# A kernel of four layers on one core: fewer full products around the score-only slots and the end of its second attention, and another order of its last sigmoids

## The chip, the cores and the metric

The kernel runs on one core of one Trainium2 chip. TensorE multiplies matrices (its clock is granted at one of two levels, 1.2 or 2.4 GHz), VectorE and ScalarE work elementwise and reduce, GpSimd (POOL in the rows) is a slower helper, and SyncE queues the transfers. The engines run their own instruction streams and wait for each other on semaphores. The metric is the device time of one execution in microseconds (us), smaller is better.

## The reference

On x of 8 samples x 256 tokens x 128 features, four layers with residuals, each behind a layer norm:

```python
x = x + attn_a(layernorm(x))     # hyperbolic-distance attention, 16 heads of 8
x = x + ffn(layernorm(x))        # 64 experts of 64, 8 of them chosen per token, and a shared one
x = x + attn_b(layernorm(x))     # softmax attention with rotary positions, 16 heads of 8
x = x + ffn(layernorm(x))        # the same experts again
...
# attn_b, per sample and head: q, k rotated
attn = softmax(einsum('qd,kd->qk', q, k) * 8 ** -0.5)
out = attn @ v
...
# routing in ffn
scores = sigmoid(x @ router_w.T)         # then grouped top-k on scores + e_bias
w = chosen scores / their sum * 2.5
```

The change lies in attn_b and in the routing of the second ffn.

## The kernel before, in words

Everything stays in on-chip memory between layers. Phase b is attn_b. prepare_b makes q and k with rotary positions in four groups of 512 tokens and, with "selection" matmuls, spreads the heads over four groups of 32 partitions each (b_qt, b_kt), as a high and a low part. samples_b then walks over 64 units of two heads of one sample, B * UNITS = 64.

Each unit goes through two kinds of score tiles. As unit V its scores are computed query by key (b_score_step), 2 heads x 2 halves of 32 x 128 weights by 256 columns, into one of three score banks (0 to 2), and VectorE reduces each head's bank to the row maxima (tensor_reduce into mx, line L2284, counted by s_mx; the matmuls count up s_s1). Every four units the maxima go through GpSimd (max_split), a transpose and a selecting matmul on TensorE (b_max_step, lines L959 and L539), ScalarE and VectorE (shift, into q2, shown as q in the rows), which subtracts them from q. AHEAD = 9 slots later, as unit U = V - 9, the shifted scores are computed key by query (b_shifted_step) into banks 3 to 5, ScalarE takes their exp (L1450, counted by s_e), and three slots later TensorE multiplies with v (pv_b, rows ps<-wr,vt).

So TensorE's slots are of three kinds. V = 3 to 8 have scores only (U = -1); they are called the lead here. U = 0 to 54 have scores and shifted scores, in four row groups at once. U = 55 to 63 have shifted scores only, and U = 64 only closes; this is the tail. In the tail and behind it (last_of_b, b_tail_step) the second ffn's router logits, its transposes and the attention's last projections are mixed into TensorE's line in an order written out by hand; on VectorE the same is written out behind its loop over V in samples_b: x_low (low part of the normalised input), marks, normalise(2) (waits for heads reloaded by transfer), sigmoids (two steps on the logits' exponentials), the last shift, the routing steps.

keep_busy(n, k) issues k full products, 128 x 128 weights by 512 columns, into a bank whose content nobody reads. They stand ahead of the selection of the last q group (8 of them, behind the scores of V = 0), behind every lead slot (3), at U = 0 to 3 (1 each), at some V where TensorE waits for the residual path (WAITS_FOR_PATH), and in the tail (TAIL_FILL, 16 in all). In the rows they are ps<-sel. All matmuls come from a helper, so their line is L539.

Of the kernel before, what the change touches and what calls it, by code (L numbers as in the profile page):

```python
# [24 lines left out]
MT = N // P  # L25
# [14 lines left out]
AHEAD = QUAD + 5  # L40
# [53 lines left out]
def hybrid(nc, x, consts, wA, wB, bqk, brow, rwT, wexp, out):  # L94
    ctx = ExitStack()

    def sem(name):
        return ctx.enter_context(nc.semaphore(name))
# [5 lines left out]
    with ctx:  # L104
# [207 lines left out]
        s_s1 = sem("b_scores_in_psum")  # L312
        s_mx = sem("b_max_read")
# [76 lines left out]
        def shifted_bank(h):  # L390

            return 3 + h % 3
# [144 lines left out]
        def _(pe):  # L537
# [274 lines left out]
            def xn_transposed_b(g):  # L812

                pe.wait_ge(s_xn, GROUPS + g + 1)
                if g >= 1:
                    pe.wait_ge(s_u, 2 * g - 1)
                for t in range(GTILES):
                    last = pe.transpose(bank(2)[:, t * P:(t + 1) * P], b_xn[g % 2][:, t, :], ident)
                last.then_inc(s_xnT, 1)
# [34 lines left out]
            def prepare_b():  # L854
                keep_busy(0, 14)
                xn_transposed_b(0)
                project_b(0)
                values_b(0)
                xn_transposed_b(1)
                for g in range(GROUPS):  # L860
                    if g + 1 < GROUPS:
                        project_b(g + 1)
                    else:
                        pe.wait_ge(s_u, 2 * GROUPS)
                        pe.wait_ge(s_vc, 2 * GROUPS)
                        b_tiles(-1, 0)
                        keep_busy(3, 8)
                        b_score_head(1, 0)
                    select_q_b(g)
                    if g + 1 < GROUPS:  # L870
                        values_b(g + 1)
                    else:
                        b_score_head(1, 1)
                        b_score_head(2, 0)
                        b_score_head(2, 1)
                    if g + 2 < GROUPS:
                        xn_transposed_b(g + 2)
                    select_k_b(g)

            def keep_busy(n, k):  # L880

                for _ in range(k):
                    mm(bank(n), sel[:, S_QH].rearrange("p c r -> p (c r)"), sel[:, :].rearrange("p s c r -> p (s c r)"))
# [7 lines left out]
            def b_shifted_step(U, mt, i):  # L891
# [2 lines left out]
                return mm(bank(shifted_bank(2 * U + i))[:, mt * N:(mt + 1) * N], b_kt[rows(j0 + i), c, tok(s, mt * P, P)],  # L894
                          q2[U // UNITS % 2][rows(j0 + i), s % 4, :], tile_position=(32 * (j0 + i), 0))

            WAITS_FOR_PATH = {20: 3, 36: 4, 41: 3, 42: 4, 52: 4, 57: 3, 58: 4}
            TAIL_FILL = {55: 1, 56: 1, 57: 1, 58: 2, 59: 2, 60: 2, 61: 1, 62: 2, 63: 1, 64: 3}

            def b_tiles(U, V):  # L900

                shifted, scores = 0 <= U < B * UNITS, V < B * UNITS
                if V == 0:
                    pe.wait_ge(s_outL, 4 * GROUPS + 2)
                    pe.wait_ge(s_outR, 3 * GROUPS + 2)
                elif V == 4:
                    pe.wait_ge(s_outL, 4 * GROUPS + 4)
                    pe.wait_ge(s_outR, 3 * GROUPS + 4)
                elif V == UNITS:
                    pe.wait_ge(s_outL, 6 * GROUPS)  # L910
                    pe.wait_ge(s_outR, 5 * GROUPS)
                if shifted and U % (UNITS // 2) == 0:
                    pe.wait_ge(s_q2, U // (UNITS // 2) + 1)
                if shifted and U >= 2:
                    pe.wait_ge(s_e, 2 * U - 2)
                if 0 <= U < 4:
                    keep_busy(shifted_bank(2 * U), 1)
                elif V in WAITS_FOR_PATH:
                    keep_busy(shifted_bank(2 * U), WAITS_FOR_PATH[V])
                elif U in TAIL_FILL:  # L920
                    keep_busy(shifted_bank(2 * U) if U <= 61 else 0, TAIL_FILL[U])
                for i in range(2):
                    if scores and 2 * V + i >= 3:
                        pe.wait_ge(s_mx, 2 * V + i - 2)
                    if shifted and i == 1 and U >= 1:
                        pe.wait_ge(s_e, 2 * U - 1)
                    for half in range(MT):
                        if scores:
                            last = b_score_step(V, half, i)
                            if half == MT - 1:  # L930
                                last.then_inc(s_s1, 1)
                        if shifted:
                            last = b_shifted_step(U, half, i)
                            if half == MT - 1:
                                last.then_inc(s_s2, 1)
# [54 lines left out]
            def samples_b():  # L990
                for V in range(3, AHEAD):
                    b_tiles(-1, V)
                    b_max_step(V)
                    keep_busy(3, 3)
                for U in range(B * UNITS + 1):
                    V = U + AHEAD
                    b_tiles(U, V)
                    if U == B * UNITS:
                        pv_b(B * UNITS // 2 - 1, 0)
                        pv_b(B * UNITS // 2 - 1, 1)  # L1000
                    elif U >= 3:
                        pv_b((U - 3) // 2, (U - 3) % 2)
                    if U == B * UNITS - 1:
                        pv_b(B * UNITS // 2 - 2, 1)
                    elif U == 55:
                        pe.wait_ge(s_mx, 2 * B * UNITS - 1)
                        logits(1, 0, 0)
                    b_max_step(V)
                    if V < B * UNITS:
                        b_path_step(V)  # L1010
                    else:
                        b_tail_step(U)
# [799 lines left out]
        def _(dve):  # L1812
# [125 lines left out]
            def sigmoids(f, i, g=None):  # L1938

                sc = route[f].sc[i] if g is None else route[f].sc[i][:, g * GTILES:(g + 1) * GTILES, :]  # L1940
                dve.wait_ge(s_sc, lap(f, i, 1 if g is None else g))
                if f == 0:
                    dve.wait_ge(s_S, CHUNKS * B - 1)
                step(dve.tensor_scalar(sc[:, :, :], sc[:, :, :], BIG, 1.0, ALU.min, ALU.add))
                step(dve.reciprocal(sc[:, :, :], sc[:, :, :]))
# [76 lines left out]
            def marks(f):  # L2022
                st.do(dve.memset(route[f].gs[:, :, 8:12], BIG))

            def x_low(f, i, g):

                dve.wait_ge(s_xh, lap(f, i, g))
                dve.tensor_tensor(xl[:, group(i, g)], f_xT[2 * i + g][:, :], xh[:, group(i, g)],
                                  ALU.subtract).then_inc(s_xl, 1)
# [249 lines left out]
            def samples_b():  # L2279
# [7 lines left out]
                def shift(k):  # L2287
                    s, half = k // 2, k % 2
                    dve.wait_ge(s_mq, k + 1)
                    if s >= 2:  # L2290
                        dve.wait_ge(s_s2, 2 * UNITS * (s - 1))
                    cs = slice(2 * half, 2 * half + 2)
                    first, chunk, _ = unit_b(UNITS * s + 4 * half)
                    dve.tensor_tensor(q2[s % 2][:, cs, :], bank(7).rearrange("p (c n) -> p c n", c=2),  # L2294
                                      b_qt[:, chunk, tok(first, 0, 2 * N)].rearrange("p (c n) -> p c n", c=2),
                                      ALU.add).then_inc(s_q2, 1)

                def normalise(c):
                    dve.wait_ge(s_old, 64 * (c + 1))
                    den = b_rden[c % 2][:, :, :].rearrange("p r j -> p j r")  # L2300
                    st.do(dve.reciprocal(den, b_rows[:, :, HD, :]))
                    st.sync()
                    if c >= 2:
                        dve.wait_ge(s_oT, B + c - 1)
                    dve.tensor_tensor(b_otok[c % 2][:, :, :].rearrange("p j (r d) -> p j r d", d=HD),  # L2305
                                      b_rows[:, :, 0:HD, :].rearrange("p j x r -> p j r x"),
                                      den.unsqueeze(3).broadcast_to([P, 4, 16, HD]), ALU.mult).then_inc(s_on, 1)
# [47 lines left out]

                x_low(1, 0, 0)
                marks(1)
                normalise(2)
                sigmoids(1, 0, 0)
                shift(2 * B - 1)  # L2360
                x_low(1, 0, 1)
                sigmoids(1, 0, 1)
                route_bests(1, 0)
                residual(2, 1)
                stats_of(2)
# [171 lines left out]
```

## Time and profile before

| what | value |
|---|---|
| median of 3 runs | 1074.56 us |
| the three runs | 1070.37, 1074.8, 1074.56 us |
| the profiled execution's own time | 1078.8 us |
| its span, first to last instruction | 1077.0 us |
| TensorE matmuls busy | 970.0 us (90%) |
| VectorE busy | 961.2 us (89%) |
| ScalarE busy | 673.4 us (63%) |
| GpSimd busy | 375.3 us (35%) |
| mean granted TensorE clock | 0.868 |

The profile is of one execution. Busy times are unions of an engine's instruction times; matmuls are pipelined, so a matmul's recorded time holds its way through the array too, and two of them overlap. A granted clock of 1.00 is 2.4 GHz and 0.50 is 1.2 GHz; a stretch's figure is the mean over it. All times in rows count from the span's start.

### The profile page before, as it was taken

How to read it: one execution, taken by the hardware profiler on the slowest of the kernel's cores; microseconds unless marked ns; L12 is line 12 of the kernel's file. 1: busy time of each engine (PE TensorE's matmuls, PEld its weight loads, DVE VectorE, ACT ScalarE, POOL GpSimd, SP SyncE). 2: the span in 40 equal slices, each digit the busy share in tenths (PEclk: the TensorE clock that was granted, in tenths of full speed). 3: DMA queues.
4: the chain of work that ended last, by engine and by line, in shares of the span. 5: the costliest groups of instructions: out<-in, count | busy, mean ns of one | idle time of the engine just before them, and what ended most of it. 6: DMA issues, size and time to landing. Idle time of an engine off the chain costs nothing. (4 is left out here: it accounts for less than half of the span.)

```text
span 1077.0 us, 17673 instructions
## 1 busy us (share of the span) xinstructions
PE 970.0 (90%) x5412; PEld 694.4 (64%) x5412; DVE 961.2 (89%) x1448; ACT 673.4 (63%) x855; POOL 375.3 (35%) x300
## 2 busy tenths in 40 slices
PE   6767888787669999999999899999999999999997
PEld 4543444444347888888888645455678888888885
DVE  7789999999988999999999797998889999999996
ACT  4779999999934545545454555877544545455453
POOL 3044666668811333334332141111203333333330
PEclk9865555555669999999999997999989999999999
DMA  2000000000108755565551000111059555555521
GB/s 59 0 2 1 1 1 1 1 1 1 52 11 201 181 150 153 151 156 143 159 148 33 1 1 1 24 24 24 23 125 230 144 158 149 153 153 151 155 69 39
DMA packets 50711, 86.94 MB, mean 81 GB/s; under 512 B 20092, under 2 KB 33404, under 8 KB 50556
## 3 DMA queue, kind: packets, MB, share of 16 engines
q1 hardware_dynamic: 50664, 86.34, 31.3%
q8 instruction: 27, 0.44, 0.2%
q14 instruction: 20, 0.16, 0.1%
HBM read 83.33 MB, written 2.98 MB: 80 GB/s over the span
## 5 line engine op out<-in xcount | busy, mean ns | idle before, releaser
L1547 ACT ACTIVATE sg<-ps 128x512 f32<-128x512 f32 x264 | 156.9, 594 | 266.2 <-PE ps L539 265.4
L539 PE MATMUL ps<-xh,whi 128*128 128x512 f32 x528 | 206.8, 392 | 1.3 <-ACT b L1366 1.3
L539 PE MATMUL ps<-xh,wlo 128*128 128x512 f32 x528 | 206.3, 391 | 0.0
L539 PE MATMUL ps<-xl,whi 128*128 128x512 f32 x528 | 206.2, 390 | 0.0
L2077 DVE TENSOR_TENSOR hf<-sg,ps 128x512 f32<-128x512 f32 x264 | 170.6, 684 | 30.0 <-DVE hl L2396 24.4
L1768 POOL CAST whi<-wraw 128x384 fp32r<-128x384 f32 x66 | 66.0, 1000 | 364.0 <-PE ps L539 285.6
L1687 POOL TENSOR_TENSOR rr<-xr,rr 128x2048 f32<-128x2048 f32 x32 | 145.2, 4568 | 125.4 <-ACT rr L1341 71.1
L2396 DVE TENSOR_TENSOR hl<-hf,hh 128x1024 fp32r<-128x1024 f32 x132 | 178.8, 1355 | 0.5 <-DVE hf L2077 0.5
L2401 DVE TENSOR_TENSOR hf<-hf,cbc 128x1024 f32<-128x1024 f32 x128 | 157.0, 1227 | 13.4
L1553 ACT ACTIVATE hh<-hf 128x1024 fp32r<-128x1024 f32 x132 | 139.1, 1054 | 4.3 <-DVE hf L2401 4.3
L1770 POOL TENSOR_TENSOR wlo<-wraw,whi 128x384 fp32r<-128x384 f32 x66 | 116.4, 1763 | 5.3
L539 PEld LDWEIGHTS ps<-xh,whi 128*128 128x128 f32 x528 | 99.7, 189 | 22.6 <-ACT b L1366 1.4
L539 PEld LDWEIGHTS ps<-xh,wlo 128*128 128x128 f32 x528 | 99.6, 189 | 21.0
L539 PEld LDWEIGHTS ps<-xl,whi 128*128 128x128 f32 x528 | 99.7, 189 | 20.7
L539 PE MATMUL ps<-hh,whi 128*128 128x512 f32 x264 | 104.2, 395 | 4.2 <-DVE hl L2396 4.2
L539 PE MATMUL ps<-hh,wlo 128*128 128x512 f32 x264 | 103.6, 392 | 0.0
L539 PE MATMUL ps<-hl,whi 128*128 128x512 f32 x264 | 103.5, 392 | 0.0
L2284 DVE TENSOR_REDUCE mx<-ps 128x2 f32<-128x512 f32 x128 | 81.1, 683 | 12.5 <-PE ps L539 11.6
L2108 DVE TENSOR_SCALAR xr<-ps 128x1024 f32<-128x1024 f32 x64 | 77.8, 1216 | 10.3 <-PE ps L539 7.4
L1450 ACT ACTIVATE wr<-ps 128x512 f32<-128x512 f32 x128 | 69.5, 599 | 27.3 <-PE ps L539 26.6
L539 PE MATMUL ps<-rr,vt 128*32 128x256 f32 x512 | 67.4, 631 | 17.0 <-ACT rr L1323 17.0
L2116 DVE SCALAR_TENSOR_TENSOR xr<-ps,xr 128x1024 f32<-128x1024 f32 x64 | 78.1, 1221 | 4.3 <-PE ps L539 0.3
(276 smaller groups left out, 1525.3 us busy)
## 6 DMA issues: line engine op xcount, KB each, us to landing
cbc<-routing_coefficients SPq DMA_DIRECT2D x256, 256.0 KB, 3.8
wraw<-in_wexp_dram SPq DMA_DIRECT2D x66, 192.0 KB, 2.7
X<-in_x_dram SPq DMA_DIRECT2D x4, 256.0 KB, 4.4
routing_coefficients<-cT SPq DMA_DIRECT2D x8, 128.0 KB, 2.3
out_dram<-X SPq DMA_DIRECT2D x4, 256.0 KB, 2.9
heads_by_row<-o_all SPq DMA_DIRECT2D x12, 72.0 KB
b_rows<-heads_by_row SPq DMA_DIRECT2D x12, 72.0 KB, 3.0
rope_in<-in_consts_dram SPq DMA_DIRECT2D x1, 512.0 KB, 3.5
```

The costliest lines, as they stand in the source:

```text
L539: return pe.matmul(o, l, r, start=start, stop=stop, **kw)
L1450: act.activation(wr[:, C % CHUNKS, h % 4 * MT * N:(h % 4 + 1) * MT * N], bank(shifted_bank(h)), ACT.Exp, scale=SCALE_B).then_inc(s_e, 1)
L1547: act.activation(sg[c % 2][:, :], bank(4 + 2 * (c % 2)), ACT.Silu).then_inc(s_sg, 1)
L1553: act.activation(hh[ring][:, :], hf[ring % 2][:, :], ACT.Copy).then_inc(s_hh, 1)
L1687: pool.tensor_tensor(rr[:, C % RR, :], xr[:, C % XR, :], rr[:, C % RR, :], ALU.add).then_inc(s_S, 1)
L1770: pool.tensor_tensor(wlo[slot][:, :], wraw[raw][:, :], whi[slot][:, :], ALU.subtract).then_inc(s_ws, 1)
L2077: dve.tensor_tensor(hf[c // 2][:, c % 2 * FF_TOK:(c % 2 + 1) * FF_TOK], sg[c % 2][:, :], bank(5 + 2 * (c % 2)), ALU.mult).then_inc(s_h1, 1)
L2108: dve.tensor_scalar(xr[:, C % XR, at], bank(0, 2), 0.0, None, ALU.max).then_inc(s_N, 1)
L2116: dve.scalar_tensor_tensor(xr[:, C % XR, at], bank(2, 2), R_MAX, xr[:, C % XR, at], ALU.min, ALU.mult).then_inc(s_X, 1)
L2284: dve.tensor_reduce(mx[U // UNITS % 2][:, c, j0 + i, :], bank(score_bank(2 * U + i)).rearrange("p (t m) -> p t m", t=MT), AX_X, ALU.max).t ...
L2396: dve.tensor_tensor(hl[ring][:, :], hf[ring % 2][:, :], hh[ring][:, :], ALU.subtract).then_inc(s_hl, 1)
L2401: dve.tensor_tensor(hf[side][:, :], hf[side][:, :], cbc[s][:, side * FF_PAIR:(side + 1) * FF_PAIR], ALU.mult).then_inc(s_h, 1)
```

## The change

It edits four places. Ahead of the last q selection, 5 full products stand instead of 8. Behind each lead slot, 2 instead of 3 (LEAD_FILL). In lead slots, both heads now wait together until the maxima up to head 2V - 2 are read, and their matmuls are issued half by half, heads by turns; before, each head waited for itself and its two halves were issued in a row. In the tail TAIL_FILL loses entries: one product less at U = 56, 57, 59 and 60, two less at U = 62. On VectorE, the sigmoids of the first logit group stand ahead of normalise(2), and those of the second ahead of x_low of that group.

```diff
                         b_tiles(-1, 0)
-                        keep_busy(3, 8)
+                        keep_busy(3, 5)
                         b_score_head(1, 0)
...
+            LEAD_FILL = {V: 2 for V in range(3, AHEAD)}
             WAITS_FOR_PATH = {20: 3, 36: 4, 41: 3, 42: 4, 52: 4, 57: 3, 58: 4}
-            TAIL_FILL = {55: 1, 56: 1, 57: 1, 58: 2, 59: 2, 60: 2, 61: 1, 62: 2, 63: 1, 64: 3}
+            TAIL_FILL = {55: 1, 58: 2, 59: 1, 60: 1, 61: 1, 63: 1, 64: 3}
...
+                if scores and not shifted and V >= 3:
+                    pe.wait_ge(s_mx, 2 * V - 1)
+                    for half in range(MT):
+                        for i in range(2):
+                            last = b_score_step(V, half, i)
+                            if half == MT - 1:
+                                last.then_inc(s_s1, 1)
+                    return
                 for i in range(2):
                     if scores and 2 * V + i >= 3:
                         pe.wait_ge(s_mx, 2 * V + i - 2)
...
                     b_max_step(V)
-                    keep_busy(3, 3)
+                    keep_busy(3, LEAD_FILL.get(V, 0))
...
                 marks(1)
+                sigmoids(1, 0, 0)
                 normalise(2)
-                sigmoids(1, 0, 0)
                 shift(2 * B - 1)
+                sigmoids(1, 0, 1)
                 x_low(1, 0, 1)
-                sigmoids(1, 0, 1)
                 route_bests(1, 0)
```

## Rows read from the trace of the kernel before

**Rows 1.** The page's costliest groups: count, then busy us, mean ns, idle before.
```profile
L1450 ACT ACTIVATE wr<-ps 128x512 f32<-128x512 f32 x128 | 69.5, 599 | 27.3 <-PE ps L539 26.6
```

**Rows 2.** Busy time by stretch: us, engines (instructions), granted clock, DMA, GB/s.
```profile
core 0: us, PE busy (x) PEld busy (x) DVE busy (x) ACT busy (x) POOL busy (x), PEclk, DMA share, GB/s
639.30:643.00 3.70, 3.70 (x18) 2.39 (x16) 3.49 (x5) 1.07 (x3) 0.86 (x1) 0.66 0.02 4
...
645.20:647.00 1.80, 1.58 (x12) 0.96 (x12) 1.11 (x2) 1.80 (x2) 1.49 (x1) 1.00 0.00 0
...
656.06:658.37 2.31, 2.31 (x8) 1.34 (x8) 1.29 (x2) 0.00 (x0) 0.12 (x1) 0.50 0.00 0
...
661.07:664.00 2.93, 2.76 (x31) 1.92 (x30) 2.39 (x4) 2.34 (x5) 0.00 (x0) 1.00 0.00 0
...
683.48:689.22 5.74, 5.41 (x68) 2.68 (x69) 5.56 (x10) 5.00 (x11) 0.70 (x5) 1.00 0.02 4
749.30:767.15 17.85, 17.84 (x164) 10.03 (x163) 13.18 (x30) 13.41 (x28) 3.13 (x7) 1.00 0.27 48
```

**Rows 3.** Timeline of the lead: start us, us, engine, line, count [idle before].
```profile
639.81 3.21 PE L539 MATMUL ps<-sel 128*128 128x512 f32 x8
...
641.31 0.69 DVE L2249 TENSOR_TENSOR b_kl<-rope,b_kh 128x512 fp32r<-128x512 f32 x1
...
642.96 0.80 PE L539 MATMUL ps<-b_qh,sel 32*128 32x512 f32 x3
...
645.24 0.50 PE L539 MATMUL ps<-b_kh,sel 32*128 32x512 f32 x2 [0.21 <-ACT b_qt L1390]
...
646.72 0.39 PE L539 MATMUL ps<-b_kt,b_qt 32*128 32x256 f32 x4
...
648.40 0.80 PE L539 MATMUL ps<-b_kt,b_qt 32*128 32x256 f32 x4
...
649.12 1.65 PE L539 MATMUL ps<-sel 128*128 128x512 f32 x3
649.23 1.29 DVE L2284 TENSOR_REDUCE mx<-ps 128x2 f32<-128x512 f32 x2 [0.79 <-PE ps L539]
...
659.10 2.05 PE L539 MATMUL ps<-sel 128*128 128x512 f32 x4
```

**Rows 4.** Timeline of TensorE, narrow windows inside one lead slot.
```profile
658.37 0.58 PE L539 MATMUL ps<-b_kt,b_qt 32*128 32x256 f32 x2
...
658.75 0.42 PE L539 MATMUL ps<-b_kt,b_qt 32*128 32x256 f32 x2
```

**Rows 5.** The chain that ended last, in order: start us, us, what.
```profile
652.12 9.47 PE ps L539 x33
...
685.13 0.37 PE ps L959 x2
...
759.88 9.28 PE ps L539 x89
```

**Rows 6.** Timeline of the tail, columns as in rows 3.
```profile
751.75 0.47 PE L539 MATMUL ps<-sel 128*128 128x512 f32 x1
751.98 0.38 ACT L1481 ACTIVATE sc<-ps 128x256 f32<-128x256 f32 x1
752.16 0.51 PE L539 MATMUL ps<-q,b_kt 32*128 32x256 f32 x4
...
754.15 0.56 DVE L2301 RECIPROCAL b_rden<-b_rows 128x64 f32<-128x64 f32 x1 [3.50 <-DMA b_rows<-heads_by_row]
...
755.68 0.29 DVE L1944 TENSOR_SCALAR sc<-sc 128x256 f32<-128x256 f32 x1
...
757.80 0.69 DVE L2294 TENSOR_TENSOR q<-ps,b_qt 128x512 fp32r<-128x512 f32 x1
...
759.23 0.66 PE L1023 MATMUL ps<-cst,b_otok 128*128 128x128 f32 x4
...
763.64 0.71 PE L539 MATMUL ps<-sel 128*128 128x512 f32 x2
764.28 0.51 PE L539 MATMUL ps<-q,b_kt 32*128 32x256 f32 x4
...
765.28 0.50 PE L539 MATMUL ps<-sel 128*128 128x512 f32 x1
```

## The prediction

> **What bounds the kernel now.** I read the page first for what phase b costs TensorE, VectorE and ScalarE [rows 1], then the stretches with their granted clock [rows 2], the order of time at the start of phase b [rows 3], the chain that ended last [rows 5] and the order of time in its last slots [rows 6]. The reader is to see three regimes.
>
> In the lead, the six slots with scores only (V = 3 to 8), TensorE never rests, the granted clock is 0.50, that is 1.2 GHz, and VectorE is busy 1.29 us of a slot of 2.31 us (the row from 656.06 is one slot [rows 2]). VectorE idles 0.79 us before a pair of maxima; TensorE has 0.80 us of scores in a slot and 1.65 us of three full products [rows 3]. So the lead is bound by its own fillers at the low clock. It lasts from 646.72 to 661.07, 14.35 us. The chain of work shows it as one piece of TensorE, 9.47 us [rows 5]. From U = 0 on the clock is 1.00 and four slots take 5.74 us; VectorE is busy 5.56 us of them, TensorE 5.41 [rows 2], but TensorE could do its own in about 4.7 (below), so VectorE binds. In the tail (U from 55) there are no scores to reduce; TensorE is busy 17.84 of 17.85 us, fillers included, at full clock [rows 2], and the chain is TensorE's for 9.28 us on end [rows 5]. The experts behind it begin when the routing behind the tail is done, so what the tail gives goes to the end.
>
> **The change part by part.**
>
> *Ahead of the selection, eight products become five.* They begin at 639.81 and the next matmuls start at 642.96 [rows 3]. A full product is 512 columns, 0.427 us at 1.2 GHz; the rows agree, as four take 2.05 us and three 1.65 [rows 3]. Three of them are 1.28 us. But the selection of q behind them also waits for b_kl on VectorE, which ends 0.69 us after 641.31, at 642.00, so it can move up only by about 0.91 us, from 642.96 to 642.05 [rows 3]. Next in line is ScalarE's copy of b_qt, which follows the selection. On the other side: the clock in 639.3 to 643.0 is 0.66 on the mean and it is 1.00 in 645.2 to 647.0 [rows 2]; it fell during the eight products and rose after them. With three fewer, and an idle wait for b_kl, I don't expect it to rise there. The selections of k and the scores of V = 3, now 645.24 to 646.72 at full clock [rows 3], and the short V = 3 slot (646.72 to 648.40, 1.68 us, against 2.31) then run at half. I price that at 1.0 us (0.5 for two selections and the scores, which stream 0.5 us and would stream twice that; 0.2 for the three fillers' part of the slot; the rest for the copies in between). Bounds: 0 if it rises anyway, 1.5 if all 1.48 us from 645.24 on double. Net of this part: 0.1 us later, between 0.9 earlier and 0.6 later.
>
> *Two products in each lead slot instead of three.* Six slots, 0.427 us each, TensorE bound: 2.56 us. Is there something that takes their place? VectorE needs 1.29 us, and the slot left is 1.88 us, so no. The new wait for all maxima up to head 2V-2 stands before both heads and behind it on TensorE are the scores, the transposes of the maxima and the fillers. It ends with the first maximum of the slot before, 0.83 + 0.69 us after that slot's scores began (649.23 less 648.40, and one of two in 1.29 us, rounded up) [rows 3]: 1.52 against 1.88, hidden by 0.36. At full clock it would be what sets the pace, at 1.3 us a slot. The shift of q that U = 0 waits for ends with VectorE's work of V = 6, three slots ahead; free.
>
> *Heads by turns.* Worth nothing. In the narrow look at one lead slot two score matmuls have started at 658.37 and cover 0.58 us together, two more cover 0.42 us from 658.75 [rows 4]: two and two, side by side, which fits one of each head, in its own row group. The Trainium skill (TensorE: Matmul & The Clock Gate, Part 3, The mechanism) says that a weight load overlaps matmuls in flight only if it goes to another row group, and that matmuls keep their order; by that rule the order of before, two matmuls of one row group in a row, should have cost up to one such step a slot, and turns should save it (rival D). The trace of before does not bear this out, as the pairs start together.
>
> *The tail, six products fewer* (16 to 10, counted in the diff: one each at U = 56, 57, 59, 60, two at 62). The sole product of a slot delays its shifted scores from 751.75 to 752.16, 0.41 us; two delay them from 763.64 to 764.28, 0.64 us, so the second is 0.23 [rows 6]. Sum: 0.41 + 0.41 + 0.23 + 0.23 + 0.64 = 1.92 us, if no wait takes over. ScalarE's two exps are 1.2 us a slot [rows 1] and the slots stay at 1.4 and more, because each also has transposes, logits or a projection. The next wait is U = 59: transposed(2) and U = 60 wait for the last shift, which runs at 757.80 for 0.69 us behind the reciprocal of the sigmoids; TensorE comes to it at 759.23 [rows 6], and 1.05 us earlier (0.41 + 0.41 + 0.23) that would be 758.18, 0.3 us too soon. That is what the new order on VectorE cures: it idles 3.50 us until the row load lands at 754.15 [rows 6], and the first sigmoids, 2.1 us (755.68 to 757.80), now fit into this gap, since their logits have been exponentiated by 752.36 [rows 6]. The shift then ends at about 756.8. x_low of group 1 moved behind the second sigmoids is not asked for until the experts; free, hidden by the wait for the projection. All of the 1.92 us count; bounds 1.2 (one wait of about 0.7 us back) and 2.2.
>
> *What the low clock does afterwards.* In the trace of before the clock came back at U = 0 (0.50 until 661, then 1.00 [rows 2]), just after four products in a row, 2.05 us [rows 3]. Now there are three there and two in each slot before it, while slots with three stayed at 0.50 here. I expect U = 0 to start at the low clock. A steady slot is at full clock 1.00 us of shifted scores and products with v (764.28 to 765.28 [rows 6]; the scores run beside the shifted ones in other row groups), and in four slots there are 0.37 us of transposed maxima [rows 5] and about as much of their selection: 4.7 us. At 1.2 GHz the scores of a slot take 0.73 us (648.40 to 649.12 [rows 3]) where a slot of the tail has about 0.43; by a ratio of 1.75 (between 1.7 and 2) the four slots take 8.2 us, against 5.74: 0.6 us a slot, TensorE then being the bound. The first three slots have no product with v and lose about 0.3 us together. From U = 3 on TensorE is nearly gapless and the clock should return within some slots; no row shows when. Nearest above is the three products at V = 20, U = 11. I take three costly slots, 0.3 + 1.8 = 2.1 us; bounds 0 (returns as before) and 0.3 + 8 x 0.6 = 5.1.
>
> **Sum**: +0.1 - 2.56 - 1.92 + 2.1 = -2.3 us. The profiled execution took 1078.8 us, 4.2 above the median of 1074.56; the runs of before span 4.4 us, much as a lead at the low or at the full clock would, so I make the sum against the profiled execution, 1076.5, and carry the difference to the median: 1072.3, said as 1072. Its own range: all bounds at their best -0.9 - 2.56 - 2.2 = -5.7, at their worst +0.6 - 2.56 - 1.2 + 5.1 = +1.9, so 1069 to 1076.5. About 0.5%, 5.4 us, is what a measurement of this kernel tells from no change: the forecast is a small gain that would not count as faster.
>
> **Rivals.** (A) The lead at full clock. If five and two products suffice to hold 2.4 GHz, VectorE sets the slot at 1.3 us: six slots 7.8 us instead of 14.35, 6.5 us saved, with 0.9 ahead and 1.9 in the tail 9.3 us. 1074.6 less 9.3 is 1065.3; as some runs of before may have had the full clock there too, I say 1066. For it: the slots get shorter, and TensorE's real work in them comes more often. Against it: TensorE was gapless in 648.4 to 661.07 and yet at 0.50 [rows 2], and two selections with copies between them, where it waits, stand just ahead. Chance 0.2.
> (B) The low clock stays, the other side. One mechanism: with fewer products the steady slots at 1.2 GHz feed the engine no more than the lead did, and the clock doesn't return until a group of fillers (V = 20, 36). Each slot costs 0.6 us; it eats the 4.4 us gain after about 7 slots, and from 16 slots on the kernel is slower by over 0.5%. Until V = 20: +1 us, 1075; until V = 36 (U = 27): 0.3 + 24 x 0.6 = 14.7, less 4.4, 1085. Chances 0.09 and 0.05.
> (C) Order within the tail: a wait takes the products' place (for exp of the slot before, or the row load for normalise, if it lands late), and the tail gives 0 to 1 us: 0.1 - 2.56 - 0.5 + 2.1 = -0.9 in all, 1073.7. Chance 0.11.
> (D) The turns do shorten the scores. The second halves start 0.38 us after the first [rows 4]; were one such step saved in each of six slots, it would be 2.3 us more: 1070. Against it: two of the four have started together already. Chance 0.05. The rule of the Trainium skill above is what speaks for it.
> The forecast keeps 0.50.
>
> **How the numbers follow.** Faster by over 0.5% (below 1069.2): most of A (0.18), half of D (0.02), and the forecast where the clock returns early (0.12): 0.32. Slower by over 0.5% (above 1079.9): late B, 0.05, and 0.02 for runs with it half the time: 0.07. The rest, 0.61, is within. The range takes in A's 1066 and early B's 1075 with the spread of the runs themselves: 1065.5 to 1077.5; late B and the far end of A, some 0.15, are left out.
>
> **What would show it.** In the profile of after: lead slots 1.9 us apart at clock 0.50 (right), 1.3 apart at 1.00 (A); the first slots from U = 0 about 2 us apart at 0.50, and where the clock returns; VectorE's idle time before its maxima down to about 0.4 us; the tail from 749.3 to 767.15 shorter by 1.9, with the shift ended before TensorE asks. It makes the prediction wrong above all if the clock behaves otherwise at U = 0, in either direction.

## The result and the profile after

The changed kernel takes 1082.11 us at the median of 13 runs (1072.86 to 1083.4), the kernel before 1074.56 us at the median of its 13 (1069.57 to 1082.1). The ratio is 1.0045, with an interval of 1.0024 to 1.0065. By the 0.5% used above that is not a clear loss, but its interval lies above 1: the gain of 2.3 us that was forecast isn't there. The profiled execution took 1083.4 us (span 1081.6), 4.6 us more than the profiled one of before (1078.8, span 1077.0). Ratios in this document leave out runs over 1.5% above a kernel's fastest; this matters for one experiment and is said there.

The page's group of the exps is as in [rows 1], now at line 1459; the change moves the lines below it by nine:

```profile
L1459 ACT ACTIVATE wr<-ps 128x512 f32<-128x512 f32 x128 | 69.5, 598 | 31.9 <-PE ps L539 31.1
```

Busy time by stretch, to be held against [rows 2]; the columns are the same:

```profile
639.30:643.00 3.70, 3.18 (x19) 1.90 (x19) 3.70 (x6) 1.22 (x2) 1.55 (x1) 1.00 0.02 4
...
653.26:655.13 1.87, 1.87 (x7) 1.00 (x6) 1.46 (x3) 0.00 (x0) 0.00 (x0) 0.50 0.00 0
661.10:664.00 2.90, 2.90 (x26) 1.64 (x25) 2.73 (x6) 1.72 (x5) 0.64 (x4) 0.50 0.00 0
664.44:672.92 8.48, 8.41 (x74) 3.68 (x70) 5.79 (x10) 5.27 (x11) 0.70 (x4) 0.50 0.01 2
684.50:690.24 5.74, 5.40 (x72) 2.68 (x68) 5.55 (x9) 4.88 (x11) 0.70 (x4) 1.00 0.00 0
...
755.07:771.41 16.34, 16.33 (x158) 9.37 (x156) 13.21 (x28) 13.41 (x28) 3.75 (x7) 1.00 0.28 53
...
644.20:681.60 37.40, 37.33 (x223) 19.63 (x223) 25.19 (x40) 17.86 (x31) 5.29 (x21) 0.50 0.00 1
681.60:705.50 23.90, 21.34 (x273) 10.55 (x266) 22.81 (x37) 20.16 (x40) 2.10 (x12) 1.00 0.22 26
```

The reader is to see the row from 644.20: 37.40 us at 0.50, the lead and eleven slots behind it, with TensorE busy for 37.33 us of it. In the kernel before, the low clock ended at U = 0. From 639.3 to 643.0 the granted clock is 1.00 now; in the kernel before its mean there was 0.66. Four slots with both kinds of scores take 8.48 us in it (the row from 664.44, U = 4 to 7) and 5.74 at full clock (from 684.50), and VectorE, which binds at full clock, is busy only 5.79 of the 8.48. The tail's stretch (from 755.07) is 16.34 us long instead of 17.85.

The timeline of the lead, TensorE and VectorE, columns as in [rows 3]:

```profile
639.12 1.43 PE L539 MATMUL ps<-sel 128*128 128x512 f32 x5
...
641.41 0.52 PE L539 MATMUL ps<-b_qh,sel 32*128 32x512 f32 x4 [0.42 <-issue]
...
646.89 0.79 PE L539 MATMUL ps<-b_kt,b_qt 32*128 32x256 f32 x4
647.62 1.22 PE L539 MATMUL ps<-sel 128*128 128x512 f32 x2
648.77 0.79 PE L539 MATMUL ps<-b_kt,b_qt 32*128 32x256 f32 x4
...
655.86 1.65 PE L539 MATMUL ps<-sel 128*128 128x512 f32 x3
```
```profile
647.72 1.29 DVE L2293 TENSOR_REDUCE mx<-ps 128x2 f32<-128x512 f32 x2 [0.59 <-PE ps L539]
```

A plain lead slot runs from 646.89 to 648.77, 1.88 us, as forecast, and VectorE's idle time ahead of its maxima is 0.59 us ("about 0.4" was forecast). Here TensorE waited 0.42 us behind the five products, before it selected q; the row names no releaser, but b_kl was done at 641.31, 0.10 us ahead of the selection's start. The clock was 1.00 then and 0.50 from 644 on.

The chain of work (start, us, what) is TensorE's from 644.17 to 686.15 but for 0.07 us; three of its pieces ahead of U = 11 are these ([rows 5]):

```profile
650.18 8.06 PE ps L539 x28
658.86 7.40 PE ps L539 x47
666.88 4.96 PE ps L539 x36
```

The timeline of the tail ([rows 6]), with the shift's chain on VectorE:

```profile
757.65 0.50 PE L539 MATMUL ps<-q,b_kt 32*128 32x256 f32 x4
...
758.50 1.75 DVE L1954 RECIPROCAL sc<-sc 128x256 f32<-128x256 f32 x1
...
760.29 0.56 DVE L2310 RECIPROCAL b_rden<-b_rows 128x64 f32<-128x64 f32 x1
...
761.85 0.68 DVE L2303 TENSOR_TENSOR q<-ps,b_qt 128x512 fp32r<-128x512 f32 x1
...
764.20 0.66 PE L1032 MATMUL ps<-cst,b_otok 128*128 128x128 f32 x4
```

The first sigmoids now run ahead of the row load's reciprocal, and the shift ends at 762.53, 1.67 us before TensorE transposes.

Where the time went is best read by stages. This table is worked out from the starts of the first score matmul of a slot (V) or its first shifted one (U) in each profile; the stages that are left out (up to V = 0, and behind U = 63) make up the rest of the span. All times are in us.

```
kernel                       V0-V3  V3-U0  U0-U4  U4-U11 U11-U27 U27-U55 U55-U63  span
before                        7.35  14.36   5.27   10.61   25.55   47.25   15.96  1077.0
after                         6.49  12.25   7.01   16.65   26.89   47.55   14.44  1081.6
three in the lead             6.99  14.81   5.26   10.61   25.55   47.28   14.45  1074.4
eight ahead                   7.34  12.02   5.95   10.61   25.55   47.24   14.45  1075.6
tail only                     7.34  14.37   5.27   10.60   25.54   48.42   14.45  1079.4
turns only                    7.34  10.27   5.27   10.60   25.54   47.28   15.96  1072.9
four at U = 0                 6.97  11.43   5.27   10.60   25.53   47.27   14.44  1070.8
none at V = 20                6.44  12.26   7.01   11.12   26.10   47.27   14.45  1075.6
no turns                      6.31  12.29   7.01   12.10   25.53   47.26   14.45  1075.8
waits filled, three           7.97   8.66   5.27   10.60   26.62   47.57   14.44  1072.3
waits filled, two             7.97   8.29   5.27   10.60   26.78   47.54   14.45  1070.4
waits filled, and the path    7.97   8.29   5.27   10.60   24.66   46.40   14.45  1067.7
  and the route               7.96   8.29   5.26   10.61   24.66   46.38   14.44  1067.6
tail's table, old order       6.41  12.51   5.27   10.61   25.55   47.26   14.89  1072.0
```

After less before: 0.68 less up to V = 0, which is not the change's; 0.86 less to V = 3, 2.11 less in the lead, 1.52 less in the tail. That is 4.5 us given. Against it stand 1.74 more in U = 0 to 3, 6.04 more in U = 4 to 10, 1.34 and 0.30 more from there to U = 55, and 0.34 behind the tail: with the 0.68 the sum is +4.6. So the gain came where it was expected, 4.5 us, and the stages with the low clock behind the lead (U = 0 to 10) took 7.78 us.

Most of the 1.34 have their own place: 0.24 us is the first slot from U = 11, in which the clock came back, and 1.09 us is the slot U = 26, where at V = 35 TensorE waits for the path. The timeline there, first of after and then of before:

```profile
705.39 0.95 PE L1032 MATMUL ps<-cst,b_otok 128*128 128x128 f32 x4 [1.55 <-DVE b_otok L2314]
705.99 2.05 PE L539 MATMUL ps<-sel 128*128 128x512 f32 x4
```
```profile
701.02 0.63 PE L1023 MATMUL ps<-cst,b_otok 128*128 128x128 f32 x4 [1.57 <-DVE b_otok L2305]
701.40 1.17 PE L539 MATMUL ps<-sel 128*128 128x512 f32 x4
```

The clock fell to 0.50 at 705.5, just behind the end of the wait, and the four products there took 2.05 us instead of the 1.17 that they take at full clock. The same wait before (1.57 us) had no such fall in its profile. The 0.30 us from U = 27 to U = 55 are the end of the same low stretch, which lasted until 709.

### The profile page after: what moved, and what is told of

The parts are those of the page before. It is cut to its first block and busy times, and to the rows that moved or that the text cites. A ratio compares the mean times of both kernels' runs of the same rounds, so it can differ in the third digit from the quotient of the medians.

```text
span 1081.6 us, 17644 instructions
## 1 busy us (share of the span) xinstructions
PE 975.0 (90%) x5397; PEld 693.3 (64%) x5397; DVE 962.9 (89%) x1448; ACT 673.9 (62%) x855; POOL 376.9 (35%) x300
```

## The experiments

Each has twelve runs, but for the last, which has one; each is named as in the table. They were taken in three sets, on three different chips: first the four of the next section; then four at U = 0, none at V = 20 and the two with the waits filled; then the rest. Every ratio is to runs of the kernel before in the same set, whose medians were 1074.98, 1075.03 and 1074.98 us.

For every single run the record also has the mean granted clock of the whole execution. It goes with the time: before's fastest runs of each set (1069.3 to 1069.7 us) have 0.878 or more, its runs above 1080 us 0.870 or less; the changed kernel has 0.871 at 1072.86 us and 0.857 to 0.862 in its eight runs above 1080.

### One part of the change undone, or done alone

**Three in the lead**: the changed kernel with the old number of products there.

```diff
-            LEAD_FILL = {V: 2 for V in range(3, AHEAD)}
+            LEAD_FILL = {V: 3 for V in range(3, AHEAD)}
```

> The changed kernel with three full products behind each lead slot again (five ahead, turns, tail and VectorE order as changed). Theory L (the low clock is carried past U = 0 because the lead has two products): the clock returns at U = 0 as in the kernel before, U = 0 to 11 take about 16 us instead of 23.7, and with the tail's 1.5 us the time is 1072 to 1074 us. Rival T (turns and the wait for both heads cost the time): about 1081 us, as the changed kernel.

Measured: 1075.22 us (1072.83 to 1080.43), ratio 0.9996 (0.9975 to 1.0018). The low clock lasted from 641 to 661.5 in its profile, so the lead was slow, but it was gone at U = 0, and U = 0 to 10 are as before (15.9 us, as expected). The time is 1.2 us above the 1072 to 1074 expected. The third figure from the right is the granted clock:

```profile
648.80:660.00 11.20, 11.20 (x38) 7.05 (x38) 6.13 (x10) 1.04 (x2) 1.33 (x8) 0.50 0.00 0
...
662.60:668.00 5.40, 4.99 (x54) 2.85 (x53) 5.40 (x10) 4.65 (x11) 0.70 (x4) 1.00 0.01 3
```

**Eight ahead**: the changed kernel with the old number ahead of the selection.

```diff
-                        keep_busy(3, 5)
+                        keep_busy(3, 8)
```

> The changed kernel with eight products ahead of the q selection again, all else as changed. Theory L with the lead's products as the cause: no better than the changed kernel, 1079 to 1082 us, the clock at 0.50 until V = 20. Theory L with the five ahead as the cause: the clock is 1.00 for part of the lead and at U = 0, 1073 us. Rival T: 1081 us, but with the clock back early.

Measured: 1077.17 us (1071.77 to 1082.18), ratio 1.0008 (0.9979 to 1.0036). The clock came back at 662.5, 2.0 us behind U = 0 (660.5), and U = 0 to 3 took 0.68 us more than before. The time lies between the two that were expected, and neither expectation had the clock as it came. Undoing either part gives most of the loss back, so neither part alone explains it.

**Tail only**: the kernel before with the tail's table and VectorE's new order.

```diff
-            TAIL_FILL = {55: 1, 56: 1, 57: 1, 58: 2, 59: 2, 60: 2, 61: 1, 62: 2, 63: 1, 64: 3}
+            TAIL_FILL = {55: 1, 58: 2, 59: 1, 60: 1, 61: 1, 63: 1, 64: 3}
...
-                normalise(2)
                 sigmoids(1, 0, 0)
+                normalise(2)
...
-                x_low(1, 0, 1)
                 sigmoids(1, 0, 1)
+                x_low(1, 0, 1)
```

> The kernel before with the tail's six products fewer and the new order of the sigmoids alone. Theory L: 1.5 us faster than before, 1073 us, and the clock in the lead and at U = 0 as before. Rival R (the tail or the order on VectorE costs time): not faster than before, 1075 us or more.

Measured: 1075.45 us, ratio 1.0011 (0.9988 to 1.0034). The tail took 14.45 us instead of 15.96, 1.51 less, in this profile as in all with the new table and the new order. The total doesn't show it: runs of one kernel differ by more, and a gain of 1.5 us would be a ratio of 0.9986, just outside the interval. In this profile a further low stretch, from 731.7 to 735.1, made U = 27 to 54 1.17 us longer.

**Turns only**: the kernel before with the heads by turns and their shared wait.

> The kernel before with heads by turns and the one wait for both heads in the lead slots alone (three products, eight ahead, tail as before). Theory L: no difference within 1 us, lead slots 2.3 us apart as before. Rival T: 3 to 7 us slower, with lead slots longer than 2.3 us. Rival D of the prediction (turns shorten the scores): up to 2.3 us faster, lead slots about 1.9 us apart.

Measured: 1074.59 us, ratio 0.9995 (0.9976 to 1.0015). In its profile the clock came back in the middle of the lead and the lead took 10.27 us, but a lead with three products and without turns also varied, between 14.37 and 12.51 us (tail only; tail's table, old order). The slot V = 4, at 0.50 almost throughout, took 2.28 us with turns, against 2.30 before. No effect of the turns is shown.

### How long the low clock lasts

**Four at U = 0**: the changed kernel, with four products in U = 0 instead of one.

```diff
-                    keep_busy(shifted_bank(2 * U), 1)
+                    keep_busy(shifted_bank(2 * U), 4 if U == 0 else 1)
```

> The changed kernel with four full products instead of one at U = 0, so that six stand in a row there (two of V = 8, four of U = 0). Theory L: three more products cost about 1.3 us at the low clock, and the clock comes back within U = 0 to 4 instead of at V = 20: U = 4 to 11 take 10.6 us instead of 16.7, and the time is 1075 to 1077 us. Rival (the low clock isn't what costs, but the order and waits of the lead): 1.3 us or more slower than the changed kernel, 1082 us and over.

Measured: 1075.75 us (1071.88 to 1077.99), ratio 0.9989 (0.9962 to 1.0016). Of the changed kernel's 13 runs 8 are above 1080 us, of these 12 none is above 1078, and none has a mean clock below 0.865. Its profile can't show the four products at work, since in that execution the clock had come back in the lead, on TensorE instructions that are those of the changed kernel up to there; only the times and mean clocks speak for the four products. (The kernel before has 8 of 34 runs above 1080 us in this set, so such times do occur on this chip.) The stretches of its profile:

```profile
645.00:650.00 5.00, 5.00 (x20) 2.87 (x18) 3.07 (x6) 3.97 (x4) 2.66 (x5) 0.50 0.00 0
650.00:655.00 5.00, 5.00 (x21) 3.04 (x20) 3.51 (x6) 0.38 (x1) 0.00 (x0) 0.54 0.00 0
655.00:660.00 5.00, 4.67 (x35) 2.90 (x31) 4.11 (x8) 1.37 (x4) 0.71 (x4) 1.00 0.00 0
```

It came back at 654.6.

**None at V = 20**: the changed kernel without the three products there (U = 11).

```diff
-            WAITS_FOR_PATH = {20: 3, 36: 4, 41: 3, 42: 4, 52: 4, 57: 3, 58: 4}
+            WAITS_FOR_PATH = {36: 4, 41: 3, 42: 4, 52: 4, 57: 3, 58: 4}
```

> The changed kernel without the three full products at V = 20 (U = 11). Theory L, that it is this group which brings the clock back in the profile of the changed kernel: the clock stays at 0.50 beyond 682 us, to the four products at V = 36 (U = 27) at the worst, at 0.8 us a slot: up to 13 us slower than the changed kernel, 1083 to 1094 us, with U = 11 to 27 up to 13 us longer. Rival (the clock returns by itself about there, products or not): 1 us faster than the changed kernel, 1080 us.

Measured: 1080.7 us (1072.07 to 1094.61), ratio 1.0001 (0.9957 to 1.0044); five of its twelve runs lie at 1089.0 to 1094.6 us and are not in the ratio. They are what matters here: no run of the changed kernel is above 1083.4, and these five have mean clocks of 0.841 to 0.849, where the changed kernel has 0.857 at the least. So without the three products at V = 20 the low clock lasted longer in some executions; how long, no profile shows. But they are not always needed. In the profile of this kernel it came back at 668.7:

```profile
660.00:665.00 5.00, 5.00 (x40) 2.64 (x36) 4.34 (x8) 3.37 (x7) 0.70 (x4) 0.50 0.00 0
665.00:670.00 5.00, 5.00 (x50) 2.37 (x52) 3.30 (x6) 2.68 (x6) 0.00 (x0) 0.63 0.02 3
670.00:675.00 5.00, 4.66 (x61) 2.21 (x53) 4.70 (x9) 4.62 (x10) 0.70 (x4) 1.00 0.00 0
```

Up to that place TensorE's instructions are those of the changed kernel, where it came back at 681.6. When it returns thus differs between executions of the same instructions.

**No turns**: the changed kernel, its two products a lead slot kept, with the old lead loop (each head waits for itself).

> The changed kernel without the heads by turns and without their shared wait; everything else as in the change. Theory L, that two products in each score slot are what leaves the granted clock at 0.50 until V=20, expects the stages from V=0 to U=11 as in the changed kernel, 42.4 us together, and some 1080 us. Theory T, that the turns are what keeps TensorE's clock low, expects the clock back near U=0, the stage from U=4 to U=11 at 10.6 us and some 1075 us.

Measured: 1079.36 us (1071.07 to 1082.32), ratio 1.0021 (0.9994 to 1.0047); 6 of 12 runs above 1080. V = 3 to U = 4 are as in the changed kernel (12.29 and 7.01 us), with the clock at 0.50; it came back at 668.8 in this profile. The clock stays low without the turns too. That the stages to U = 11 would be as long as in the changed kernel (42.4 us) did not come true in this execution: they took 37.7.

### Holding the full clock

**Waits filled, three**: before's numbers of products, the new tail, and products where TensorE waits between the selections. **Waits filled, two**: the changed kernel with eight ahead and the same products in the waits. The first three lines stand between the halves of select_k_b, for the last two groups of tokens, the last line behind the scores of V = 2's second head.

```diff
+                if g >= GROUPS - 2:
+                    pe.wait_ge(s_u, 2 * GROUPS)
+                    keep_busy(3, 2)
...
                         b_score_head(2, 1)
+                        keep_busy(3, 4)
```

> The kernel before with the changed tail and VectorE order, eight ahead and three in each lead slot, and with full products in the waits ahead of the lead, where TensorE idles: two between the halves of the k selections of groups 2 and 3, four behind the scores of V = 2. Theory L: the clock stays at 1.00 from 637 us through the lead, VectorE sets the lead slots at 1.3 us, V = 3 to U = 0 takes 8 us instead of 14.4, and the time is 1067 to 1070 us. Rival (the clock falls in the lead whatever stands ahead): 1073 to 1075 us, lead slots 2.3 us apart at 0.50.

> The changed kernel (two products in lead slots, turns, tail) with eight ahead and the same products in the waits ahead of the lead. Theory L: if the clock is at 1.00 when the lead begins, slots of 1.3 us with two products hold it there, as its slots are then short: 1067 to 1070 us, no different from three in each slot. Rival (two are too few at any clock): it falls in the lead, comes back only at V = 20, 1080 us.

Measured: with three 1074.03 us, ratio 0.998 (0.9953 to 1.0008); with two 1072.19 us (1069.87 to 1074.58), ratio 0.996 (0.9933 to 0.9988). In both profiles the clock is 1.00 throughout the lead, which takes 8.66 and 8.29 us instead of 14.36 and 12.25. The stretches and the timeline of the one with two:

```profile
647.00:655.40 8.40, 7.42 (x49) 4.18 (x45) 7.77 (x13) 2.87 (x4) 1.42 (x8) 1.00 0.00 0
...
695.00:699.00 4.00, 3.70 (x24) 2.57 (x24) 1.52 (x4) 0.67 (x2) 0.71 (x4) 0.57 0.00 0
```
```profile
648.36 0.50 PE L539 MATMUL ps<-b_kt,b_qt 32*128 32x256 f32 x4 [0.21 <-DVE mx L2297]
...
654.05 0.50 PE L539 MATMUL ps<-b_kt,b_qt 32*128 32x256 f32 x4 [0.68 <-DVE mx L2297]
```

Two things are to be seen. At full clock and with two products the lead is VectorE's: TensorE waits for the maxima. (With three, TensorE was busy for 8.00 of the 8 us from 648, and the lead is 0.37 us longer.) And with two products a slot the clock stayed at 1.00, as it did with three. But it fell at 695.2, behind the wait at V = 35, with three at 696.4. The clock and the lead came as expected, the times didn't, by 2 to 4 us (1067 to 1070 was expected for both): U = 11 to 26 took 1.23 and 1.07 us more than before, and V = 0 to 2, where the new products stand, 7.97 us instead of 7.34, though at full clock. So those products were not free. And of the twelve runs with three, two still took 1079.65 and 1081.2 us, at a mean clock of 0.868 and 0.869.

**Waits filled, and the path**: six products stand in that wait, at V = 35 and at V = 51, and the four in the score stream behind each are gone. **And the route**: nine products instead of three ahead of the last logits, and two behind them.

```diff
-            WAITS_FOR_PATH = {20: 3, 36: 4, 41: 3, 42: 4, 52: 4, 57: 3, 58: 4}
+            WAITS_FOR_PATH = {20: 3, 41: 3, 42: 4, 57: 3, 58: 4}
...
                     pe.wait_ge(s_q2, V // QUAD)
+                    pe.wait_ge(s_e, 2 * (V - AHEAD))
+                    keep_busy(shifted_bank(2 * (V - AHEAD + 1)), 6)
                     pe.wait_ge(s_on, B + c + 1)
```

> As the kernel of this batch with both parts, but with the part at V=35 and V=51 alone. My theory expects about 1.8 us from the eight products taken off the path and about 1.1 from the low stretch near 695 us: 1069 to 1070 us, and 1.00 granted from the first score slot to the end of the score stage. The rival (the products in the wait push the scores behind them) expects about 1072 us.

> The changed kernel with eight slots ahead and products in the waits of the selection, as in the run before this one of that kind (1072.2 us), and in addition: at V=35 and V=51 six products stand in the wait that VectorE's score path already has (about 1.6 us idle there) instead of four in the middle of the score stream, and the last projection matmuls of the route have nine products ahead of them instead of three and two behind (idle 1.6 and 0.8 us). My theory, that the granted clock falls to 0.50 after waits of TensorE and that every product on the path costs its own time, expects about 1.8 us from the eight products taken off the path, about 1.1 from the low stretch near 695 us that goes, and 0.5 to 1.5 from one low stretch less at 777 to 784: 1067.5 to 1070 us. The rival, that products in a wait delay what follows them as much as they give back, expects about 1072 us, no gain on that kernel.

Measured: with the path alone 1070.17 us (1069.39 to 1071.26), ratio 0.9939 (0.9915 to 0.9962), the lowest median here, and faster than before by its interval. The gain is in the median: before's fastest run of that set took 1069.46 us, about as long as the fastest with the path (1069.39), but its runs go up to 1082.41 and these only to 1071.26. It is 1070.43 us (1069.33 to 1074.29) with the route as well, ratio 0.9955 (0.9929 to 0.9981). The path came as expected, the route is worth nothing: the low stretch from 783.4 stands in both profiles. U = 11 to 55 took 71.06 us against 74.32 without this part, 3.3 less. The profile of before, with no low stretch at that place and the same fillers, took 72.80; so about 1.7 us of it goes with the eight products that are off the path, and about 1.5 with the low stretch. The timeline shows both:

```profile
693.42 1.65 PE L539 MATMUL ps<-sel 128*128 128x512 f32 x6
695.09 0.63 PE L1036 MATMUL ps<-cst,b_otok 128*128 128x128 f32 x4
```
```profile
693.88 1.06 DVE L2320 TENSOR_TENSOR b_otok<-b_rows,b_rden 128x512 f32<-128x512 f32 x1
```
```profile
695.00:699.00 4.00, 3.98 (x51) 2.33 (x54) 3.70 (x7) 3.01 (x6) 0.70 (x4) 1.00 0.00 0
```

The transposes start right behind the sixth product, 0.15 us after b_otok is there (694.94), as long after it as without the products (0.14 us in the kernel with two), and the scores behind them run at once and at full clock.

**Tail's table, old order**: the kernel before with the new TAIL_FILL and VectorE's old order of sigmoids, one run. (It is six products fewer, not five.)

> The kernel before with only the five full products less at the end (the table for U=56 to 62), and VectorE's old order of the last sigmoids. The prediction's step said that in this order the shifts would bind where products are gone. That expects the stage from U=55 to U=63 at 14.75 us or more, against 14.45 in the run that had both edits and 15.96 before. The rival, that the order of the sigmoids doesn't matter, expects 14.45.

Measured: 14.89 us for U = 55 to 62, against 14.45, and 1073.86 us in its one run. The timeline names the wait:

```profile
756.47 0.66 PE L1023 MATMUL ps<-cst,b_otok 128*128 128x128 f32 x4 [0.37 <-DVE q L2294]
```

The transposes of U = 59 wait 0.37 us for the last shift. The old order costs 0.44 us of the tail here.

## Why the prediction was wrong

Forecast were 1072 us, within 1065.5 to 1077.5; measured were 1082.11.

**The step that failed** is "I take three costly slots, 0.3 + 1.8 = 2.1 us". The mechanism up to there was the right one: U = 0 starts at the low clock, and a steady slot then is TensorE's. What failed is how soon the clock returns, and what a slot costs until then. The clock stayed low for eleven slots in the profiled execution, up to the three products at V = 20; this is rival B's first case, which had a chance of 0.09 and a time of 1075. It was priced too low also: the bound 0.3 + 8 x 0.6 = 5.1 us for this place stands against 7.78. The first three slots lost 1.60 us, not 0.3 (they take 5.12 us, 657.44 to 662.56, against 3.52, 661.08 to 664.60): the forecast let the missing product with v cover almost all of it. The next eight lost 0.69 each on average, not 0.6 (four of them take 8.48 us, against 5.74 for four at full clock). And the three products at V = 20 themselves took 0.69 us more (1.58 from the first to the next scores, against 0.90). Together 1.60 + 8 x 0.69 + 0.69 = 7.8. With 7.8 in place of 2.1 the sum is +3.4. Behind it come 0.24 in U = 11, and 1.10 + 0.30 in the second low stretch, at V = 35, for which no term stood. The rest is small: 0.5 less ahead of and in the lead than forecast, 0.4 more in the tail, 0.68 less up to V = 0 and 0.34 more behind the tail. That makes the +4.6.

How long the low clock lasts differs between executions. In the no-turns kernel and the one without V = 20 the clock came back at 668.8 and 668.7 in their profiles and took 1077.6 and 1077.3 us; the changed kernel, at 681.6, took 1083.4, and 8 of its 13 runs lie above 1080. The failure isn't bad luck with one profile: the median run, 1082.11 us, has the same mean clock as the profiled one, 0.859. The step rested on one passage of before, where the clock returned behind four products; "nearly gapless" was taken as enough to bring it back "within some slots". The same trace had the counter-evidence, which the prediction itself used against rival A: TensorE without a gap at 0.50 for the whole lead [rows 2].

**The carry to the median.** The working took the profiled execution 4.2 us above the median of before and kept that distance. After's own profiled run is 1.3 above its median, so median against median the loss reads as 7.6 us, by the ratio 4.8, and in the profiled pair 4.6. Before's runs fall in groups near 1069.5, 1074.5 and 1082; one run of each is a poor base for a term of 2 us.

**Ahead of the selection.** Forecast 0.91 earlier, then 1.0 later. V = 0 to V = 3 gave 0.86, TensorE being held 0.42 us by a wait as expected. Of the 1.0 only 0.46 came: V = 3 took 1.71 us against 1.68 with three products, instead of 0.43 less. So the part is 0.40 us earlier in all, not 0.1 later, inside its bounds. The course of the clock was another than forecast, though: it didn't fall during the products and stay down, but was 1.00 up to 644.1 and fell there.

**The lead.** Forecast 6 x 0.427 = 2.56, measured 2.11, five times 0.42; the sixth is V = 3, counted above. The slot of 1.88 us is as forecast. VectorE's idle time of 0.59 us is what that slot leaves behind 1.29 us of maxima; the "about 0.4" came from the 0.79 us of one row, where a slot of 2.31 us leaves 1.02. Rival A was wrong in this execution, but the runs with the waits filled show its mechanism: at full clock the lead takes 8.29 us, where 7.8 was forecast, with VectorE as the bound. In these profiles the clock did not fall ahead of the lead, and then it stayed, with two products a slot as with three.

**Heads by turns.** Worth nothing, as forecast: both experiments on it agree (leads of 12.29 and 12.25 us without and with turns; the scores of a slot at 0.50 cover 0.80 us without and 0.79 with), rival D is out. The Trainium skill's rule on row groups (TensorE: Matmul & The Clock Gate, Part 3, The mechanism), which spoke for D, found nothing to save, since the pairs had started together before.

**The tail.** Forecast 1.92, measured 1.51, inside the bounds. The term that was too large is the sole product of U = 56 and U = 57, 0.41: each saved 0.28 and 0.29 (slots of 2.12 and 2.21 us against 2.40 and 2.50). By the starts of single matmuls the shifted scores of U = 56 now start 0.205 us behind the last matmul of the logits (757.446 and 757.651), where the full product of before started 0.084 us behind it (751.669 and 751.753); the delay that a product makes in its row doesn't show this. At U = 62 it was 0.47 for two, not 0.64, by the same. The new order on VectorE did what was said, and is worth 0.44 us; the wait predicted as 0.3 us was 0.37 in the one run with the old order. Rival C is out.

**Open.** Why undoing either of two parts (three in the lead; eight ahead) brings the time back, and which of the two weighs more: 1075.22 and 1077.17 us lie within each other's spread. What decides in an execution whether the clock returns at 654.6, 668.7 or 681.6 wasn't isolated either, nor was the mechanism by which the clock returns at all. The low stretches behind 777 us occur in every profile; the one attempt at them failed.

## What to carry to other kernels

Price a filler by the clock that it holds for what follows, not by its own length: in the profiled execution 2.1 us were saved in the lead and 7.8 us lost behind it, where the next stage had real work to slow down. If a stage begins right behind waits of TensorE, try the fillers in those waits, and take them out of the busy stretches. At V = 35 six products in the wait delayed nothing; between the selections and ahead of V = 3 they cost 0.6 us. All of it together, with the shorter tail, gave 0.6% in the median, and none of its twelve runs was above 1071.3 us. And when one execution shows where a clock came back, take that place as one draw of several, and price the next group of fillers as an end that may well come.

## What the runs showed of the hardware

TensorE can be busy without a gap and stay at the lower clock for long: in the changed kernel it was at 0.50 for 37.40 us from 644.2 on, busy for 37.33 of them, with scores of 32 rows, small matmuls and none to two full products a slot; with the same slots the clock stayed at 1.00 from 647 to 695 in the profile of the changed kernel with the waits filled. Behind a wait of 1.55 us it fell (705.5 in the changed kernel), behind one of 1.57 us in the profile of before it didn't. The Trainium skill (TensorE: Matmul & The Clock Gate, Part 1: The HAM clock gate) says that the gate follows how busy the engine has been recently and that sustained work releases it. The trace disagrees in so far as busy time by the profile is no measure of it; the page also says that the place of the transition varies from run to run, by about half a microsecond. The three profiles that returned at 654.6, 668.7 and 681.6 on the same instructions agree that it varies, but by 27 us.

The same lead got either clock for different parts of it in different executions of the same TensorE instructions: three products a slot took 14.37 us in one profile and 12.51 in another. Over whole executions, the runs of the kernel before spread from 1069.6 to 1082.1 us, and the slower ones have the lower mean clock (0.878 to 0.881 at the fast end, 0.863 to 0.870 above 1080). That is more than most edits here are worth; in which stages the unprofiled runs differ isn't on record.
